# Cross-attention: K and V projected in three one-pass products from high and low halves, V for two steps at once

## The reference

```python
def _attn(xq, ctx, wq, wkv, wo, bo):
    q = _heads(xq @ wq)                       # 16 heads of 64
    k, v = jnp.split(ctx @ wkv, 2, axis=-1)   # ctx: 8 x 1601 x 96, wkv: 96 x 2048
    k = _heads(k); v = _heads(v)
    q = _rope(q, ...); k = _rope(k, ...)
    a = jax.nn.softmax(jnp.einsum('bhnd,bhmd->bhnm', q, k) * DH ** -0.5, axis=-1)
    o = jnp.einsum('bhnm,bhmd->bhnd', a, v)
    return o.transpose(0, 2, 1, 3).reshape(...) @ wo + bo

ctx_n = _ln(context, ca_lnc_w, ca_lnc_b)
x = _attn(cross_in, ctx_n, ca_wq, ca_wkv, ca_wo, ca_bo) + x
```

## Time and profile before

| | |
|---|---|
| median of three runs | 1933.79 us |
| span of the profiled execution | 1934.6 us |
| self-attention, about | 0 to 385 us |
| passage to cross-attention, about | 385 to 457 us |
| cross-attention in its steady order | 457 to 1862 us |
| PE busy / PEld busy / DVE busy, whole span | 98% / 67% / 82% |
| ACT busy / POOL busy, whole span | 49% / 65% |

### The profile page before, as it was taken

How to read it: one execution, slowest core, us unless ns; L and a number is a source line. 1 busy time by engine, 2 the same in 40 slices (tenths; PEclk the granted TensorE clock), 3 DMA queues, 4 the chain that set the end, 5 groups by cost and what they waited for, 6 DMA issues and landing times.

```text
span 1934.6 us, 52084 instructions
## 1 busy us (share of the span) xinstructions
PE 1889.5 (98%) x19952; PEld 1289.2 (67%) x19952; DVE 1582.3 (82%) x2316; ACT 945.2 (49%) x1460; POOL 1266.3 (65%) x816
## 2 busy tenths in 40 slices
PE   7999999979999999999999999999999999999999
PEld 5666767745666666666666666666666666666664
DVE  4999999967888888888888888888888888888842
ACT  3555545533545444445554445455444445544444
POOL 4777756415776676677767677776776667667661
PEclk8999999978999999999999999999999999999999
DMA  5332233211111111111111111111111111111100
GB/s 176 117 88 86 81 112 88 73 33 48 53 54 53 55 51 53 59 55 54 54 51 55 52 58 57 51 56 51 55 50 56 57 54 56 51 53 52 53 29 23
DMA packets 147729, 119.07 MB, mean 62 GB/s; under 512 B 63392, under 2 KB 111648, under 8 KB 147488
## 3 DMA queue, kind: packets, MB, share of 16 engines
q1 hardware_dynamic: 110624, 115.46, 17.9%
q10 hardware_dynamic: 36864, 0.28, 1.0%
HBM read 36.71 MB, written 1.05 MB: 20 GB/s over the span
## 4 chain that ended last, share of the span: by engine, by line
PE 87%; POOL 4%; issue 3%; DVE 3%; DMA 1%; ACT 1%; SPq 0%; ACTq 0%; DVEq 0%; POOLq 0%
PE S L1376 24%; PE OB L1390 20%; PE PB L1338 10%; PE PB L1325 10%; PE S L1357 7%; PE PB L1399 2%; PE PB L1310 2%; PE S L1225 2%; PE PB L1409 1%; PE PB L1191 1%; PE OB L1253 1%; PE OB L1236 1%; DMA swapped<-turned 1%; POOL KL L667 1%; POOL psum_acc L674 1%
## 5 line engine op out<-in xcount | busy, mean ns | idle before, releaser
L708 POOL TENSOR_TENSOR psum_acc<-psum_acc,P 124x1024 f32<-124x1024 f32 (+1 forms) x320 | 689.8, 2156 | 216.9 <-ACT P L851 207.4
L851 ACT ACTIVATE P<-S 124x1024 f32<-124x1024 f32 (+1 forms) x448 | 431.3, 963 | 514.6 <-PE S L1376 513.9
L1069 DVE TENSOR_REDUCE mxc<-S 128x2 f32<-128x1024 f32 x384 | 470.0, 1224 | 94.9 <-PE S L1357 88.1
L1390 PE MATMUL OB<-P,V 124*64 124x256 f32 (+1 forms) x3328 | 437.3, 387 | 0.0
L1390 PEld LDWEIGHTS OB<-P,V 124*64 124x64 f32 (+1 forms) x3328 | 221.4, 137 | 188.7 <-issue 104.8
L701 POOL TENSOR_TENSOR psum_acc<-P 124x1024 f32<-124x1024 f32 x64 | 152.0, 2374 | 213.4 <-ACT P L851 213.4
L1376 PE MATMUL S<-QH,KH 64*124 64x256 f32 (+1 forms) x1664 | 271.8, 323 | 5.8 <-ACT P L851 5.8
L728 ACT ACTIVATE V<-PB 124x512 f32<-124x512 f32 (+1 forms) x320 | 157.2, 491 | 206.4 <-PE PB L1338 167.0
L1376 PEld LDWEIGHTS S<-QH,KH 64*124 64x124 f32 (+1 forms) x1664 | 154.0, 181 | 128.5 <-issue 104.7
L1376 PE MATMUL S<-QL,KH 64*124 64x256 f32 (+1 forms) x1664 | 235.2, 278 | 0.0
L1376 PE MATMUL S<-MX,share 64*124 64x256 f32 (+1 forms) x1664 | 235.0, 278 | 0.0
(11 more groups left out here) (159 smaller groups left out, 2844.8 us busy)
## 6 DMA issues: line engine op xcount, KB each, us to landing
swapped<-turned SPq DMA_DIRECT2D x512, 128.0 KB, 2.1
kv_w<-sa_kv_dram SPq DMA_DIRECT2D x64, 128.0 KB, 2.3
qswapped<-qturned SPq DMA_DIRECT2D x128, 64.0 KB, 1.9
kv_w<-ca_kv_dram SPq DMA_DIRECT2D x64, 96.0 KB, 2.2
ctxT_all<-ctx_dram SPq DMA_DIRECT2D x8, 624.0 KB, 4.4
q_w<-sa_wq_dram SPq DMA_DIRECT2D x64, 64.0 KB, 2.0
q_w<-ca_wq_dram SPq DMA_DIRECT2D x64, 64.0 KB, 2.0
o_w<-ca_wo_dram SPq DMA_DIRECT2D x64, 64.0 KB, 2.0
```

Of the source, the lines that this page charges most:

```text
L708: pool.tensor_tensor(acc, acc, P_of(J, c)[0:rows, :, 0:w], ALU.add).then_inc(x.acc, 1)
L851: act.activation(P_of(J, c)[0:rows, :, 0:w], SP[0:rows, :, 0:w], ACT.Exp, scale=SCALE).then_inc(x.e, 1)
L1069: dve.tensor_reduce(mxc[:, t, :, c:c + 1], MP[:, :, 0:w], AX.X, ALU.max).then_inc(x.am, 1)
L1390: ins = pe.matmul(OB[half(h), 0:N], Vb[J % 2][0:w, t, half(h)], P_of(J, c)[0:w, h, k * N:(k + 1) * N], start=(t == 0), stop=(t == len(a_.t ...
```

## The change

The normalised context and the K and V weights are split into a high part (rounded to fp32r by ACT) and a low part (the rest, by POOL). The weights of the eight pairs are split once, 96x512 in one tile `wsplit` with four blocks of 128 columns: K high, K low, V high, V low. The context is split per batch in four chunks (`xh` on ACT, `xl` on POOL), the first batch within self-attention and each next one during the steps of the batch before. The per-step load of the K and V weights is gone.

A K chunk is now three full fp32r products (weights low with context high, high with high, high with low) of 512 or 66 columns. V is projected for two steps at once: for each tile three full fp32r products with 256 columns, the V weights of two pairs. The groups of V are the 7 units of two tiles; an even step's order does `v0` to `v3` (units 0 to 3 of two steps), an odd step's `v0` to `v2` (units 4 to 6, the last a single tile). ACT reads each group by two copies, one for each step, and V has three buffers instead of two, QH and QL three instead of four. TensorE's and ACT's orders change as follows; DVE's does not change.

```diff
-                  "a4 k1+1 p2+-1 v3+-1 a5 n0 s4+-1 q+1 p3+-1 a6 s5+-1 p4+-1 v0 k2+1 n1 p5+-1 s6+-1 a0+1 v1 n2 s0 "
-                  "a1+1 p6+-1 k3+1 v2 n3 s1 a2+1 sum+-1 k0+2 n4 s2 a3+1 p0 p1 o+-1 s3",
+                  "a4 k1+1 v0+1 p2+-1 a5 n0 s4+-1 q+1 p3+-1 a6 s5+-1 v1+1 k2+1 p4+-1 n1 p5+-1 s6+-1 a0+1 v2+1 n2 s0 "
+                  "a1+1 k3+1 v3+1 p6+-1 n3 s1 a2+1 k0+2 sum+-1 n4 s2 a3+1 p0 p1 o+-1 s3",
...
-                  "e1+-1 e2+-1 kh3 e3+-1 ve3+-1 e4+-1 kh0+1 e5+-1 mr ve0 n0 qh+1 e6+-1 kh1+1 ve1 n1 e0 kh2+1 ve2 "
-                  "oe+-1 n2",
-                  "c4+-1 qa+1 c5+-1 cf+-1 c6+-1 ql+1 c1 c2 c3",
-                  "w+2 k0+1 k1+1 q+1 wo k2+1 k3+1")
+                  "wh+3 e1+-1 e2+-1 kh3 e3+-1 ve0+1 e4+-1 kh0+1 e5+-1 mr ve1+1 n0 qh+1 e6+-1 kh1+1 ve2+1 n1 e0 kh2+1 ve3+1 "
+                  "oe+-1 n2 xh",
+                  "c4+-1 qa+1 c5+-1 cf+-1 c6+-1 ql+1 wl+3 c1 xl c2 c3",
+                  "r+4 w+2 k0+1 k1+1 q+1 wo k2+1 k3+1")
...
-            for dst, source in ((condT, cT_in), (ada, ada_in), (cols, cols_in), (ident, ident_in)):
+            for dst, source in ((condT, cT_in), (ada, ada_in), (cols, cols_in), (ident, ident_in), (cols96, cols96_in)):
...
+            def low_context(b, k):
+
+                lo, w = a_.chunks[k]
+                pool.wait_ge(x.xh, b * NK + k + 1)
+                pool.tensor_tensor(ctxL[:, b * M + lo:b * M + lo + w], ctxT_all[0:DC, b * M + lo:b * M + lo + w],
+                                   ctxH[b % 2][:, lo:lo + w].bitcast(F32), ALU.subtract).then_inc(x.xl, 1)
...
-                    copy(Vb[J % 2][0:w, ts[0]:ts[-1] + 1, :],
-                         XB[0:w, 0:len(ts) * PAIR].rearrange("p (t n) -> p t n", n=PAIR)).then_inc(x.ve, 1)
+                    wait(act, x.vp, n)
+                    wait(act, x.pv, (2 * m - 2) * NU + g + 1)
+                    for i in range(2):
+                        ins = copy(V_of(2 * m + i, ts[0], ts[-1] + 1)[0:w],
+                                   XB[0:w, 0:len(ts) * 2 * PAIR].rearrange("p (t i n) -> p t i n", i=2, n=PAIR)[:, :, i, :])
+                    ins.then_inc(x.ve, 1)
...
-                    for h in range(2):
-                        ins = pe.matmul(KB[c % 2][half(h), 0:w], kv_w[J % UNROLL][0:DC, half(h)],
-                                        ctxT_all[0:DC, at:at + w], start=True, stop=True)
+                    high, low = ctxH[b % 2][:, lo - o:lo + w], ctxL[:, b * M + lo - o:b * M + lo + w]
+                    terms = ((1, high), (0, high), (0, low))
+                    for n, (part, context) in enumerate(terms):
+                        ins = pe.matmul(KB[c % 2][:, 0:w + o], wsplit[:, p, part * PAIR:(part + 1) * PAIR], context,
+                                        start=(n == 0), stop=(n == len(terms) - 1))
                     ins.then_inc(x.kp, 1)
...
-                        for a, b in ((0, DH), (DH, w)):
-                            ins = pe.matmul(XB[a:b, k * PAIR:(k + 1) * PAIR], ctxT_all[0:DC, lo + a:lo + b],
-                                            kv_w[J % UNROLL][0:DC, PAIR:2 * PAIR], start=True, stop=True)
+                        high, low = ctxH[b % 2][:, lo:lo + w], ctxL[:, b * M + lo:b * M + lo + w]
+                        terms = ((low, 2), (high, 2), (high, 3))
+                        for n, (context, part) in enumerate(terms):
+                            ins = pe.matmul(XB[0:w, i * 2 * PAIR:(i + 1) * 2 * PAIR], context,
+                                            wsplit[:, p:p + 2, part * PAIR:(part + 1) * PAIR],
+                                            start=(n == 0), stop=(n == len(terms) - 1))
                     ins.then_inc(x.vp, 1)
```

More of the change, by code:

```diff
@@ L217, in __init__ @@
             def __init__(self):
-                self.load = [sem(f"ctx_loaded{b}") for b in range(B)]
+                self.load = [sem(f"ctx_loaded{i}") for i in range(LOADS)]
                 self.tree = sem("ctx_tree")
@@ L262, in __init__ @@
                 self.w = [sem(f"{n}_weights_loaded{i}") for i in range(UNROLL)]
+                self.raw = [sem(f"{n}_kv_weights_loaded{i}") for i in range(UNROLL)]
+                self.wh = sem(n + "_kv_weights_high")
+                self.wl = sem(n + "_kv_weights_low")
+                self.xh = sem(n + "_context_high")
+                self.xl = sem(n + "_context_low")
                 self.wo = [sem(f"{n}_wo_loaded{i}") for i in range(UNROLL)]
@@ L354, in q_free @@
         def q_free(eng, J):
-            wait(eng, x.s, times(J, NU) - (UNROLL - 1) * NU)
+            wait(eng, x.s, times(J, NU) - (QSLOTS - 1) * NU)
         def P_of(J, c):
@@ L383, in max_to_rows, with v_group, V_of, k_bank @@
                               ).then_inc(semaphore, 16)
+        def v_group(J, k):
+            m, g = J // 2, J % 2 * 4 + k
+            return (m, g, m * NU + g + 1) if g < NU else None
+        def V_of(J, lo, hi):
+            if J % 3 < 2:
+                return Vb[J % 3][:, lo:hi, :]
+            if hi <= 10:
+                return tree_room[:, lo * PAIR:hi * PAIR].rearrange("p (t n) -> p t n", n=PAIR)
+            return o_room[:, UNROLL + lo - 10:UNROLL + hi - 10, :]
+        def k_bank(c):
+            w = a_.chunks[c][1]
+            return KB[c % 2][:, w % 2:w % 2 + w]
+        def raw_weights(p):
+            return (qswapped[1] if p == 0 else qturned[1] if p == 1 else kv_w[p % UNROLL])[0:DC, :]
+        def both_parts(weights):
+            return weights.rearrange("p (a n) -> p a n", n=PAIR)
+        def split_of(p, low):
+            return wsplit[:, p, :].rearrange("p (a l n) -> p a l n", l=2, n=PAIR)[:, :, low, :]
+        SPLIT = 50
+        def context_split(J):
+            b, k = J // PAIRS + 1, J % PAIRS - 1
+            return (b, k) if b < B and 0 <= k < NK else None
         def halves(tile):
@@ L728, in copy, with high_weights, high_context @@
                 return act.activation(out, in_, ACT.Copy)
+            def high_weights(p, _):
+                if p < PAIRS:
+                    act.wait_ge(x.raw[p % UNROLL], p // UNROLL * 16 + 16)
+                    if p >= PAIRS // 2:
+                        wait(act, z.y, STEPS // 2)
+                    copy(split_of(p, 0), both_parts(raw_weights(p))).then_inc(x.wh, 1)
+            def high_context(b, k):
+                lo, w = a_.chunks[k]
+                act.wait_ge(cx.done, b * CG + k + 1)
+                if b > 1:
+                    wait(act, x.kp, (b - 1) * PAIRS * NK)
+                    wait(act, x.vp, (b - 1) * PAIRS // 2 * NU)
+                copy(ctxH[b % 2][:, lo:lo + w], ctxT_all[0:DC, b * M + lo:b * M + lo + w]).then_inc(x.xh, 1)
             def norm(ln, by=""):
@@ L1291, in cross_words, with split @@
                 uses = x_uses(a_, ahead(*RAMP_PE.values(), RAMP))
[L1293 removed]
+                readers = {"q": (x.qc, lambda K, k: K + 1), "v": (x.ve, lambda K, k: v_group(K, k) and v_group(K, k)[2]),
                            "sum": (x.ot, lambda K, k: K + 1),
                            "o": (x.added, lambda K, k: K + 1)}
[L1297 to L1298 removed]
+                def split(J, g):
+                    wait(pe, x.wl, min(J, PAIRS - 1) + 1)
+                    wait(pe, x.xl, batch(J) * NK + g + 1)
                 def project_q(J, _):
[L1301 removed]
+                    wait(pe, x.w[J % UNROLL], J // UNROLL * 16 + 16)
                     if J == 0:
@@ L1315, in project_k @@
                     lo, w = a_.chunks[c]
-                    at = batch(J) * M + lo
-                    loaded(J)
+                    o, b, p = w % 2, batch(J), J % PAIRS
+                    split(J, c)
                     wait(pe, x.kl, times(J, NK) + c - 1)
@@ new lines, in project_k, with project_v @@
+                    terms = ((1, high), (0, high), (0, low))
+                    for n, (part, context) in enumerate(terms):
+                        ins = pe.matmul(KB[c % 2][:, 0:w + o], wsplit[:, p, part * PAIR:(part + 1) * PAIR], context,
+                                        start=(n == 0), stop=(n == len(terms) - 1))
+                    ins.then_inc(x.kp, 1)
+                def project_v(J, k):
+                    if v_group(J, k) is None:
+                        return
+                    m, g, n = v_group(J, k)
+                    b, p = batch(2 * m), 2 * m % PAIRS
+                    wait(pe, x.wl, min(2 * m + 1, PAIRS - 1) + 1)
+                    wait(pe, x.xl, b * NK + (sum(a_.tiles[a_.units[g][-1]]) - 1) // a_.chunks[0][1] + 1)
@@ L1384, in products @@
                             wait(pe, LN2.std, 1)
-                    wait(pe, x.ve, times(J, NV) + a_.units[c][-1] // 4 + 1)
+                    wait(pe, x.ve, J // 2 * NU + c + 1)
                     wait(pe, x.e, times(J, NU) + c + 1)
```

162 lines of the change are left out of this document (97 added, 65 removed), and 4 rows, old and new, of the table SELF.

## The result

The changed kernel takes 1941.05 us (median of seven runs, 1938.22 to 1944.69); the kernel before took 1933.79 (seven runs, 1930.18 to 1937.10). The ratio is 1.0040, with a 95% interval of 1.0028 to 1.0052. So it is slower by 7 us, beyond the 0.2% that count as a change. The forecast was 1926, faster: its sign is wrong, and the time lies 1 us above the range. Two of the ten executions of one experiment, `pure`, took 2042.44 and 2235.81 us at granted clocks of 0.84 and 0.75 and are left out of its median and ratio.

The account below looks back on a forecast made before the run. TensorE was taken to bound the kernel, at 22.64 us a step. Streaming -1.01 and switches +0.89 gave -0.12 us a step, -8 us over 62.5 steps; waits counted as nothing: 1926 us, range 1878 to 1940.

Parts of the forecast that it names:

- Added 4.52, saved 1.01: K and V streaming on TensorE per step: 5.53 us removed, 4.52 added, 1.01 saved (0.93 to 1.12).
- their term: TensorE's shape switches per step: 14 costing 2.45 us become 18 costing 3.34, so 0.89 us added.
- the waits, which I had outside the sum: TensorE's waits on other engines: nothing in the sum; margins missed by 0.2 us every second step would add 6 us.
- `s0` on the exponential of `s6`: Odd steps: score bank free 1.37 us after `s6` began, TensorE's list takes 1.43, so free by 0.06 us.
- The price of a switch: Each TensorE shape change: 0.10 us, then the first weights, about 0.05 for 64 columns and 0.10 for 128.
- full and row halves are two modes: Switches between full and row halves, six per step: bounds nothing and 0.21 us, taken as 0.21.
- Rival B: Full fp32r products' weights are not loaded under the product before: +2.2 us a step, +136 us, 2070; chance 0.06.
- Rival C: First weights of full products, and of row halves after one, load within the switch: -45 us, 1889; chance 0.08.
- The alternation of even and odd steps: Cross steps with eight and five V tiles alternate at 23.03 and 22.01 us, mean 22.52.
- `v1` behind `qc`: `v1`, straight after `s5`, waits for `qc` to free XB: 0.15 us of slack.
- 5 us in all 32: POOL's added context subtractions, four per 8 steps: nothing, or 5 us in all if POOL had no room.
- 0.75 for faster: Chances for the measured time: faster 0.75, same 0.14, slower 0.11.

Follow-up runs that it names:

- pure: Changed kernel reordered so each gap between row halves holds only full products or only column halves, V tiles 6 and 7: 1938.09 us, 1.0016 of the kernel before.
- balanced: Changed kernel with V's single last tile moved, so steps have 7 and 6 V tiles instead of 8 and 5: 1934.41 us, 0.9992 of the kernel before.
- split_group: Changed kernel with p2 moved between k1 and v0, splitting one group of full products in two: 1949.56 us, 1.0067 of the kernel before.
- products: Whole block left out; only TensorE products in runs of one kind and alternations, other engines idle, then busy; 512-column fp32r products 0.228 us apart.

## Why the prediction was wrong

**The first failing step is the term "Added 4.52, saved 1.01".** The one-pass products were priced at 0.215 for 512 columns and 0.114 for 256. They take 0.233 and 0.118, in the changed kernel and nearly so by themselves (0.228, 0.120): 9 x 0.018 = +0.16 for K and 39 x 0.004 / 2 = +0.08 for V per step. The short chunk gives back 0.09. With its first load it was priced at 0.37 + 0.107 = 0.48; it takes 0.33 in odd steps, where column halves follow (1039.15 to 1039.57, less the switch), and 0.44 on the mean in even steps, counting in that V's first product behind it comes 0.08 late. Net +0.15 us, so the products save 0.86 and not 1.01. The V bound of 0.118 was in the range of that term, but K's 0.215 had no range at all, though the rows had it: `a5` to `s4`, 0.35 (1203.98 to 1204.33), is a fp32r product of 512 columns with a load of 0.107, so 0.24. I had read it as "0.22 and a little", taking an fp32 pass's rate for a product of another type.

The switches came out slightly better than their term. The mean step without waits is 22.59, 0.05 below the 22.64 before; with 0.86 saved by the products that leaves +0.81 for the switches, where I had 0.89. A change of shape takes 0.09 and the load behind it 0.10, where I had 0.10 and 0.107. So TensorE's own work gained 0.05 us a step of the forecast 0.12, some 3 us, which a measurement of this kernel could not tell from nothing. By kinds of step it closes too: even steps took 23.18 where 23.03 was forecast, odd ones without their waits 22.00 where it was 22.01.

**The second failing step is the waits, which I had outside the sum, and it turned the sign.** The prediction named `s0` on the exponential of `s6`, found 0.06 us of margin and put a miss of 0.2 into the upper range. Both lengths were right: the exponential ended 1.37 us after `s6` began (1036.18 to 1037.55), and the list needs 1.43. Left out was the time from its end to the start of `s0`, 0.14: `s0` began 1.51 after `s6`, a wait of 0.08. All waits together were 0.31 per odd step, 0.155 on the mean, with `k3` on `kl1` among them, which I had not named: +9.5 us over 61 steps, more than the gain. The errors, 0.15 - 0.08 + 0.155, are 0.23 us a step, which is what the mean step missed by: 22.75 - 22.52. balanced shows the part of the waits: without most of them the kernel equals the one before, it isn't slower.

**What held.** The price of a switch: 0.09 and the first weights, in the trace and in split_group, and that full and row halves are two modes, for which no row stood; in products that switch took 0.20 to 0.21 and a change of type nothing. By the Trainium skill's "TensorEngine Tiling (Array Packing)", Key Properties, a change of mode drains the engine, and products agrees; of the operand's type that section says nothing. Rival B's rule is contradicted for fp32r as for fp32: full products with a load each stand 0.228 us apart. The Trainium skill states that rule in "TensorE: Matmul & The Clock Gate", The mechanism, though the section's first paragraph also lets a load into the background weight buffer go ahead of running products, and that reading fits these runs. Rival C (the load within the switch) holds in one case only, the short chunk. The alternation of even and odd steps came too, 23.18 and 22.31. I priced `v1` behind `qc`: it didn't wait in the changed kernel. POOL, SP and the start cost nothing that shows: POOL is busy 1005.84 us of the stretch, 25 more than before, and no row of PE's waits in that stretch names it. My bound for a POOL without room, "5 us in all 32", was that of one batch: 32 subtractions of 1.28 are 41 us.

The margin should have decided the chances. A forecast of -0.12 us a step, left over from -1.01 and +0.89, with a rate in it that no row showed, was 8 us with an error of that size or more; 0.75 for faster was too much.

## What to carry to other kernels

Where the gain is a difference of two large terms, take each rate from a row of the same operand type, and give every one a range. Before a product changes its shape, count the runs of each shape in the order: a gap between two runs should hold one shape only, and that regrouping was worth more here (some 0.6 us a step) than the change of the products as it was made. Work that is done for two steps at once should still be spread evenly over them. A margin between two engines must hold the time from the end on one to the start on the other, 0.14 us here, before it counts as free; and a word that waits must not stand in front of one that is ready, as the copy of K did in front of `e0`.

## What the runs showed of the hardware

- A one-pass fp32r product streams 6 to 10% slower than a bf16 one: 0.228 to 0.235 us against 0.216 for 512 columns, 0.118 to 0.120 against 0.109 for 256, in full and row-half shape alike (products, and the changed kernel).
- Changing the operand type within one shape costs nothing (3.26 us for a cycle of 6 x 0.429 + 3 x 0.228).
- A change among full, row halves and column halves costs 0.09 to 0.10 us and the load of the first weights (0.05 for 64 columns, 0.10 to 0.11 for 128), in every pair tried in products. Three products of 66 columns behind such a change take 0.36 us together, no more than their own three loads; the product of 256 columns behind them is 0.07 late (1016.51 to 1016.70, 0.19 where 0.12 is usual).
- `s0` started 0.14 us behind the end of the exponential that it waited for, and `k3` 0.15 behind the end of `kl1`.
- A wait in front of a product may expose a load too: in pure `a1` started late for `am0` by 0.05 us, and the product behind it stood another 0.11 later. The 0.11 is the size of a load of 128 columns; that it is that load is an inference.
